# Linear-attention layers with centred weights, the residual on TensorE and f32r parts

## What is computed

```
q = phi(h @ wq + bq);  k = phi(h @ wk + bk);  v = h @ wv + bv
kv = sum over the sequence of k v;  z = 1 / (q . sum of k + 1e-6)
att = q kv z                                  (per head)
h = ln(h + att @ wo + bo, g1, be1)
y = gelu(h @ w1 + c1) @ w2 + c2
h = ln(h + y, g2, be2)
```

## Time and profile before

| | us |
|---|---|
| median of three runs | 2196.71 |
| lowest, highest | 2192.24, 2207.43 |
| profiled execution, its own time | 2191.62 |
| its span in the trace | 2189.9 |
| TensorE busy | 1866.5 |
| VectorE busy | 1437.3 |
| ScalarE busy | 1302.0 |
| GpSimd busy | 581.3 |

### The profile page before, as it was taken

The page is one execution under the profiler, slowest core; times in us unless marked ns, Lnnn a source line. Parts: engine busy times, 40 slices in busy tenths (PEclk is TensorE's granted clock), DMA queues, the critical chain, the costliest instruction groups (busy, mean ns, idle before and its releaser), DMA issues.

```text
span 2189.9 us, 23815 instructions
## 1 busy us (share of the span) xinstructions
PE 1866.5 (85%) x8305; PEld 1056.7 (48%) x8324; DVE 1437.3 (66%) x2318; ACT 1302.0 (59%) x2022; POOL 581.3 (27%) x685
## 2 busy tenths in 40 slices
PE   8999999999999989998677777997677677777998
PEld 6886444344434437885233334784122323332786
DVE  6886564456445647886755653886899755662787
ACT  6997555555555558997255556555644535556554
POOL 1443000000000002443522222222599612223221
PEclk9999999999999999999689998998799779999999
DMA  3221000000000002220000000200000000000110
GB/s 97 79 69 56 1 17 17 0 17 17 17 0 17 10 10 71 71 73 29 1 1 1 1 1 1 78 29 0 10 3 31 1 1 1 1 1 1 52 55 19
DMA packets 23746, 52.39 MB, mean 24 GB/s; under 512 B 2336, under 2 KB 6816, under 8 KB 23648
## 3 DMA queue, kind: packets, MB, share of 16 engines
q1 hardware_dynamic: 23648, 51.12, 7.3%
HBM read 49.47 MB, written 1.64 MB: 23 GB/s over the span
## 4 chain that ended last, share of the span: by engine, by line
PE 57%; DVE 21%; ACT 14%; issue 4%; POOL 2%; DMA 1%; ACTq 0%; POOLq 0%; DVEq 0%; SPq 0%
PE ps L440 9%; PE ps L442 9%; PE ps L441 9%; PE ps L708 5%; DVE arena L1463 5%; PE ps L225 4%; DVE arena L1208 4%; PE ps L701 4%; PE ps L928 3%; PE ps L898 3%; ACT rstd L242 2%; PE ps L887 2%; ACT arena L990 2%; ACT arena L1040 2%; ACT rstd L238 2%
## 5 line engine op out<-in xcount | busy, mean ns | idle before, releaser
L548 DVE TENSOR_TENSOR hid_lo<-arena,hid_hi 128x512 fp32r<-128x512 f32 x384 | 340.6, 900 | 67.1 <-ACT arena L498 64.7
L526 POOL TENSOR_TENSOR w_lo<-wslot,w_hi 128x512 fp32r<-128x512 f32 x56 | 77.5, 1389 | 759.4 <-DVE w_hi L543 759.4
L1208 DVE TENSOR_REDUCE arena<-ps 128x1 f32<-128x512 f32 (+3 forms) x352 | 213.2, 638 | 88.8 <-PE ps L902 85.7
L440 PE MATMUL ps<-x_hi,w_hi 128*128 128x512 f32 x512 | 208.1, 406 | 0.6 <-DVE arena L630 0.6
L441 PE MATMUL ps<-x_lo,w_hi 128*128 128x512 f32 x512 | 205.2, 401 | 0.0
L442 PE MATMUL ps<-x_hi,w_lo 128*128 128x512 f32 x512 | 205.0, 400 | 0.0
L495 ACT ACTIVATE hid_hi<-ps,wslot 128x512 fp32r<-128x512 f32 x256 | 177.1, 692 | 34.1 <-PE ps L442 6.3
L1040 ACT ACTIVATE arena<-ps 128x1024 f32<-128x1024 f32 (+3 forms) x256 | 166.5, 706 | 48.5 <-PE ps L918 47.9
L1126 POOL TENSOR_SCALAR_AFFINE_SELECT arena<-arena 128x256 f32<-128x256 f32 x256 | 102.2, 406 | 330.7 <-ACT arena L1040 328.2
L898 PE MATMUL ps<-arena 128*128 128x128 bf16 (+3 forms) x498 | 132.5, 332 | 65.3 <-DVE arena L1208 37.1
L498 ACT ACTIVATE arena<-ps,wslot 128x512 f32<-128x512 f32 x256 | 175.1, 684 | 0.0
(11 more groups left out here) (225 smaller groups left out, 3863.7 us busy)
## 6 DMA issues: line engine op xcount, KB each, us to landing
arena<-gates_dram SPq DMA_DIRECT2D x96, 256.0 KB, 3.5
wslot<-pack_a SPq DMA_DIRECT2D x16, 514.5 KB, 3.7
wslot<-pack_b SPq DMA_DIRECT2D x8, 901.5 KB, 4.6
wslot<-pack_c SPq DMA_DIRECT2D x8, 768.0 KB, 4.5
res<-x_in SPq DMA_DIRECT2D x4, 256.0 KB, 4.5
out_dram<-res SPq DMA_DIRECT2D x4, 256.0 KB, 2.9
bc_dram<-arena SPq DMA_DIRECT2D x1, 384.0 KB, 3.2
arena<-bc_dram SPq DMA_DIRECT2D x16, 24.0 KB
```

The lines of the kernel that those rows point to most:

```text
L440: pe.matmul(ps[:, bank, :], w1, hi, start=start, stop=False)
L548: dve.tensor_tensor(hid_lo[item % 2][:, k, :], hid32[:, k, :], hid_hi[item % 2][:, k, :].bitcast(F32), ALU.subtract).then_inc(S["hid_ok"], 1)
L1208: dve.tensor_reduce(neg_max[:, i, heads[0]:heads[-1] + 1:step], ps[:, bank, 0:len(heads) * keys].rearrange("p (m k) -> p m k", k=keys), AX ...
```

## The change

The layers are written out one after the other instead of looped, and the work of a layer is arranged anew.

- The residual goes through TensorE. The matrix `cent` (identity minus 1/128) is applied to the old state in two f32r parts (`centred`, two matmuls per sequence), and the product of the branch is added in PSUM. VectorE subtracts the row means from Wo and W2 once per layer (`weights`, steps 0 and 1), the biases bo and c2 are centred by one small matmul. What stands in PSUM is then already without its mean, and the norms have no mean matmul and no subtraction.
- Wo is folded into each sequence's key-value block: transpose (`kvt`), copy, a product of 128 columns with Wo (`g`), copy. The queries are multiplied by the spread reciprocals, and one matmul per sequence gives the branch. The denominators lie as 128 x 256, so that the reciprocal has 256 columns.
- The middle norm's variances of the four sequences stand in four strips of one bank; one Ln and one Exp serve all, and four matmuls with `pick` spread the root.
- Queries, up and down matmuls are three f32r matmuls each (`split3`). High parts of the state are written by ScalarE, low parts of the middle state by VectorE, low parts of the layer's output and of the weights by POOL (`pool_layers`, new). Gelu parts: for even pieces ScalarE writes gelu twice (f32r and f32), for odd pieces VectorE copies; VectorE subtracts.
- Order: keys and values of a sequence go ahead of its queries; up and down matmuls alternate piece by piece; the closing norm's variances stand between them, and that of the fourth sequence behind the next layer's first keys.
- SP's wait ahead of a layer's weights is now for the outputs of the layer that used the slot.

```diff
+            def split3(bank, w_at, s, hi, lo, lo_ready, stop, start=False):
+                w1, w2 = (t[s][:, w_at:w_at + P] for t in (wb_hi, w_lo))
+                pe.matmul(ps[:, bank, :], w1, hi, start=start, stop=False)
+                pe.matmul(ps[:, bank, :], w2, hi, start=False, stop=False)
+                lo_ready()
+                return pe.matmul(ps[:, bank, :], w1, lo, start=False, stop=stop)
...
+            def centred(bank, hi, lo, stop):
+                pe.matmul(ps[:, bank, :], cent_r[:, :], hi, start=True, stop=False)
+                return pe.matmul(ps[:, bank, :], cent_r[:, :], lo, start=False, stop=stop)
...
+                pe.wait_ge(S["w_parts"], c["parts"] + 2 * l + 2)
+                keys_values(0)
+                if l:
+                    last_var(l - 1)
+                queries(0)
+                queries(1)
+                keys_values(1)
+                queries(2)
+                keys_values(2)
+                queries(3)
+                keys_values(3)
+                for b in range(NB):
+                    pe.wait_ge(S["kf_ok"], m + b + 1)
...
+                for b in range(NB):
+                    pe.wait_ge(S["kvbd_ok"], m + b + 1)
+                    pe.transpose(ps[:, b, 256:256 + P], kv_bd[:, b, :], ident).then_inc(S["kvt_mm"], 1)
...
+                for b in range(NB):
+                    pe.wait_ge(S["kvt_ok"], m + b + 1)
+                    pe.matmul(ps[:, b, 384:384 + P], kv_t[:, b, :], w[:, B_WO:B_WO + P], start=True,
+                              stop=True).then_inc(S["g_mm"], 1)
...
+                def residual(b):
+                    pe.wait_ge(S["g_ok"], m + b + 1)
+                    centred(b, h_hi[:, b, :], h_lo[:, b, :], False)
...
+                pe.wait_ge(S["root_ok"], 2 * l + 2)
+                for b in range(NB):
+                    pe.matmul(ps[:, 4 + b, :], ccol("pick")[32 * b:32 * b + 32], root[32 * b:32 * b + 32, :],
+                              start=True, stop=True).then_inc(S["root_bc"], 1)
...
+                        pe.wait_ge(S["gelu_ok"], 16 * l + n - 2)
+                    split3(n % 3, B_W1 + k * P, s, mid_hi[:, b, :], mid_lo[:, b, :],
+                           lambda: pe.wait_ge(S["mid_lo_ok"], m + b + 1), True, True).then_inc(S["ff1_mm"], 1)
...
+                def ff2(b, k):
+                    if k == 0:
+                        centred(4 + b, mid_hi[:, b, :], mid_lo[:, b, :], False)
+                    pe.wait_ge(S["gelu_lo"], 16 * l + FC * b + k + 1)
+                    mm = split3(4 + b, B_W2 + k * P, s, hb_b[b % 2][:, k, :], lb_b[b % 2][:, k, :],
...
+                for item in range(NB + 1):
+                    for k in range(FC):
+                        if item < NB:
+                            ff1(item, k)
+                        if item:
+                            ff2(item - 1, k)
+                        if item == 2 and k == 1:
+                            pe.wait_ge(S["mid_xc"], m + 4)
+                            var(l, 0, LN2_BANK[0])
+                        if item == NB and k < 2:
+                            pe.wait_ge(S["gelu_ok"], 16 * l + 14 + k)
+                            var(l, 1 + k, LN2_BANK[1 + k])
...
+                mid_high(0)
+                mid_high(1)
+                gelu(0, 0)
+                mid_high(2)
+                mid_high(3)
+                gelu(0, 1)
+                gelu(0, 2)
+                gelu(0, 3)
+                for b in range(1, NB):
+                    for k in range(FC):
+                        gelu(b, k)
+                        if b >= 2 and k == 0:
+                            square(b - 2)
+                act.preload_act_table_set("natural_log_exp_and_others")
+                root_of(l, 0, LN2_BANK[0])
+                square(2)
+                root_of(l, 1, LN2_BANK[1])
+                out_high(l, 0, w)
+                root_of(l, 2, LN2_BANK[2])
+                out_high(l, 1, w)
+                square(3)
+                out_high(l, 2, w)
...
+            def weights(l, step):
+                s = l % 2
+                if step == 0:
+                    dve.wait_ge(S[f"w_in{s}"], w_count(c, l))
+                    square_w = wslot[:, s, B_WO:B_KVB].rearrange("p (a n) -> p a n", n=P)
...
+                    square_w = wslot[:, s, B_WO:B_KVB].rearrange("p (a n) -> p a n", n=P)
+                    dve.wait_ge(S["w_prep"], 2 * l + 1)
+                    dve.scalar_tensor_tensor(out=square_w, in0=w_sum[:, :].unsqueeze(2).to_broadcast([P, 1 + FC, P]),
+                                             scalar=-1.0 / P, in1=square_w, op0=ALU.mult,
...
+                    dve.wait_ge(S["w_prep"], 2 * l + 2)
+                    dve.tensor_copy(wb_hi[s][:, a:b], wslot[:, s, a:b]).then_inc(S["w_hi_ok"], 1)
+            def scaled(l, b, bank, bias):
+                dve.wait_ge(S["brs_ok"], 4 * l + b + 1)
+                dve.scalar_tensor_tensor(out=rstd[:, b, :], in0=ps[:, bank, :], scalar=bias, in1=rstd[:, b, :],
...
+                keys_values(0)
+                if l:
+                    scaled(l - 1, 3, 7, c_bias[:, LAYERS + l - 1:LAYERS + l])
+                    shifted(2 * m - 4, 3, ha, before[:, B_G2:B_G2 + 1], before[:, B_BE2:B_BE2 + 1], S["h_ok"])
+                queries(0)
+                queries(1)
+                keys(0)
+                keys_values(1)
+                queries(2)
+                keys_values(2)
+                keys(1)
+                queries(3)
+                keys_values(3)
+                keys(2)
+                keys(3)
...
+                if l + 1 < LAYERS:
+                    weights(l + 1, 0)
+                dve.wait_ge(S["den_ok"], l + 1)
+                dve.reciprocal(rz, rz).then_inc(S["rz_ok"], 1)
+                if l + 1 < LAYERS:
+                    weights(l + 1, 1)
...
+                    dve.wait_ge(S["gelu_ok"], n + 1)
+                    if b >= 2:
+                        dve.wait_ge(S["ff2_mm"], m + b - 1)
+                    if k % 2:
+                        dve.tensor_copy(hb_b[b % 2][:, k, :], hid_g[:, b % 2, k, :]).then_inc(S["gelu_hi"], 1)
+                        dve.wait_ge(S["gelu_hi"], 8 * l + 2 * b + k // 2 + 1)
+                    dve.tensor_tensor(lb_b[b % 2][:, k, :], hid_g[:, b % 2, k, :],
+                                      hb_b[b % 2][:, k, :].bitcast(F32), ALU.subtract).then_inc(S["gelu_lo"], 1)
...
+                for b in range(NB):
+                    for k in range(FC):
+                        gelu_low(b, k)
+                        if l + 1 < LAYERS and b == 1 and k % 2:
+                            weights(l + 1, 2 + k // 2)
+                c2 = c_bias[:, LAYERS + l:LAYERS + l + 1]
+                for b in range(NB - 1):
+                    scaled(l, b, 4 + b, c2)
+                    shifted(2 * m + 4, b, ha, w[:, B_G2:B_G2 + 1], w[:, B_BE2:B_BE2 + 1], S["h_ok"])
...
+            def weights(l, cut):
+                s, (a, b) = l % 2, CUTS[cut]
+                pool.wait_ge(S["w_hi_ok"], c["parts"] + 2 * l + cut + 1)
+                pool.tensor_tensor(w_lo[s][:, a:b], wslot[:, s, a:b], wb_hi[s][:, a:b].bitcast(F32),
+                                   ALU.subtract).then_inc(S["w_parts"], 1)
...
+                pool.tensor_tensor(h_lo[:, b, :], ha[:, b, :], h_hi[:, b, :].bitcast(F32),
+                                   ALU.subtract).then_inc(S["h_lo_ok"], 1)
...
+            for l in range(LAYERS):
+                for b in range(NB):
+                    low(l, b)
+                if l + 1 < LAYERS:
+                    weights(l + 1, 0)
+                    weights(l + 1, 1)
...
-            with sp.Fori(1, LAYERS // 2) as r:
-                l = 2 * r
-                for s in range(2):
-                    sp.wait_ge(S["ln_out"], 4 * (n0 + 2 * (l + s) - 4) + 8)
-                    sp.dma_start(wslot[:, s, 0:B_COLS], pairs[s, r]).then_inc(S[f"w_in{s}"], 16)
...
+            for l in range(LAYERS):
+                s = l % 2
+                if l < 2:
+                    slot_free(sp, s)
+                else:
+                    sp.wait_ge(S["h_hi_ok"], 4 * l)
+                    sp.wait_ge(S["h_ok"], 4 * l - 4)
+                sp.dma_start(wslot[:, s, 0:B_COLS], pack_b[l]).then_inc(S[f"w_in{s}"], 16)
```

480 lines of the change are left out of this document (303 added, 177 removed).

## The result

The changed kernel takes 2146.44 us (median of 4 runs, 2143.80 to 2149.48) against 2202.07 (4 runs of the kernel before, 2192.24 to 2208.88). The ratio is 0.975, with a 95% interval of 0.970 to 0.980. The forecast was 2132, its range 2110 to 2154. The profiled execution took 2143.8 (span 2142.1) against 2191.6.

The account below looks back on a forecast made before the run. TensorE was taken to bound stage B, the linear-attention layers, except at norms and a reciprocal. Start +9.4, cold clock +2, seven periods -68.0, tail -6.3 give -62.9: 2128.7 us, 2133.8 as median, taken as 2132 (2110 to 2154).

Parts of the forecast that it names:

- first period, with the cold clock: Stage's first layer: 61.3 us, with nothing left over from a layer before, plus 2 for a clock pause.
- tail: Stage's end, behind the seven periods: 81.7 us against 88.0, so -6.3.
- Keys, queries and their products: Head of each layer: 15.4 us of TensorE work plus 3.2 of waits, 18.6 against 17.6.
- Attention: Attention part of each layer: Wo folded in, reciprocal halved to about 1.7 us; 9.5 against 11.25.
- Middle norm: Norm ahead of the feed-forward: no mean or subtraction, one Ln and Exp for all sequences; 5.9 us against 7.59.
- Feed-forward: Feed-forward of each layer: split matmuls 22.2 us, residual 1.9, three variances 2.6, waits 2.5; 29.2 against 28.54.
- Closing norm: Layer's end: hidden behind the last feed-forward products and the next layer's first keys; 7.6 us of the gain.
- A: Rival: clock falls once per layer, in the middle norm; 14 us at most, 2146; chance 0.13 at its long end.
- B: Rival: the clock doesn't come back before the feed-forward ends; a layer takes 74.3 us, the kernel 2220; chance 0.04.
- C: Rival: POOL's six low parts all on the path, +8.1 us a layer, 2197, no change; chance 0.05.
- D: Rival: VectorE and ScalarE keep up better, the head's 3.2 us of waits go; 2106; chance 0.05.
- The prediction's own signs: In the layers: wrong if split matmuls stand further apart, clock is under 0.95, or POOL waits exceed 0.5 us a layer.

Follow-up runs that it names:

- e1_fill: The changed kernel with idle f32r products added where TensorE waits in the middle norm; 2144.71 us (2 runs).
- e7_border_fill: e3_norm_back with idle products added where TensorE waits at the layer's border and in the middle norm; 2167.4 us (2 runs).
- e3_norm_back: The changed kernel with the last sequence's variance, root and output put ahead of the next layer's first keys; 2183.61 us (10 runs), ratio to before 0.993.
- e4_f32_ff: The changed kernel with one f32 product in place of three f32r ones in the feed-forward, parts still made; 2185.01 us (7 runs), ratio to before 0.994.
- e6_pool_twice: The changed kernel with another, unread subtraction ahead of each of POOL's in the layers; six periods average 65.80 us against the changed kernel's 64.40.
- e5_before_again: The kernel before, unchanged, profiled once more; stage B 603.38 us from norm to norm, against 603.45 in its first profile.

## Why the prediction was right, and where it was off

The direction, the size and the mechanism held. From profiled execution to profiled execution 15.1 us are missing (2143.8 against 2128.7): 5.0 in stage B and 10.1 in the stages that the change doesn't touch. In the median 14 are missing (2146.4 against 2132).

| term | forecast | measured | from |
|---|---|---|---|
| first keys later | +9.4 | +8.8 | 17.57 (227.83 - 210.26) against 8.80 |
| first period, with the cold clock | 61.3 + 2 | 63.13 | its row |
| six periods | 63.2 each | 64.40 each | 386.43 / 6 |
| tail | 81.7 | 80.26 | 757.65 - 677.39 |
| stage B | -62.9 | -57.9 | 547.39 against 605.26 |
| all other stages | 0 | +10.1 | -47.8 of span |

1. *Keys, queries and their products:* 18.76 for 18.6, with the waits where they were put (1.02 ahead of the third product, 1.3 forecast). Right.
2. *Attention:* 9.12 for 9.5. The reciprocal's size was right; its wait is 0.37, not 0.7. The doubled reciprocal shows that its cover is used up.
3. *Middle norm:* 6.14 for 5.9, with one Ln and Exp. The mechanism is right; the terms that the prediction lists for it add up to 5.7, not to the 5.9 that it uses.
4. *Feed-forward:* this is the term that was mis-sized, 30.5 to the forecast's 29.2. In e1_fill, at full clock, the period is 64.0 and its feed-forward 29.9, so 0.7 is missing without any clock. The waits at its start were put at 2.5 and come to 2.1 (4.85 from the first to the fifth up product, less twelve products at 0.231). What was left out is the wait for the third sequence's square, 0.7 idle and 0.85 by the starts around it. The rest is the products' spacing, 0.234 (35 of them from 267.20 to 275.38) where 0.231 was laid out, a hundred times over. The clock adds 0.4 on average.
5. *Closing norm:* that it can be hidden is confirmed, what it is worth alone is not. The prediction put 7.6 of the 9.3 on this norm. The border, where the fourth sequence's part is hidden, is worth 3.6 a layer plus the clock (e7_border_fill, e3_norm_back), and the f32r products are worth 4.9 (e4_f32_ff). That second gain is in the prediction's own sum (32 products at 0.86 are 27.5, in place of them 22.2), but its marks hid it, since the residual and the three variances moved into the same 29 us. The two together are 8.5, a little more than the 8.2 that a layer gained. It isn't shown what the first three sequences' roots behind the feed-forward, the missing means and the single Ln and Exp are worth, nor what the added work costs; no run undoes one of these alone.

*First period and start:* the prediction let the first layer be 1.9 shorter than the rest, as nothing is left over from a layer before, and put 2 us of cold clock on top. The 63.13 measured is close to that 63.3, but the two terms can't be told apart. The cold clock is there: sequence 0's keys take 3.2 (227.83 to 231.05), those of sequence 1 take 1.5 (232.66 to 234.20). How much of these 1.7 the waits behind them take up, no run shows. The tail's 81.7 stands in the prediction without a working; 80.26 was measured.

*Rivals.* A happened, in seven layers of eight, with the mechanism named and both prices in or next to the ranges given (0.15 for 3.4 us, 0.5 to 0.8 for 6.8, and 0.1 more by e1_fill's own delay). That the kernel came out at A's 2146 is chance: A has 14 us of falls in the stage, and they cost some 2.3. B did not happen: the clock came back within 6.8 us each time. Its price was too high as well. It lets half clock cost half its length, so that 18 us a layer decide; in e3_norm_back 16 us cost 3.4 against e7_border_fill, a fifth of their length. C is excluded by e6_pool_twice, and no wait of TensorE for POOL stands in the changed kernel's six periods. D did not happen; the head's waits are all there.

*The prediction's own signs:* none of those that would have proved it wrong came. The clock over the six periods is 0.96; in the three with a long fall it is 0.947, just under the 0.95 that it names.

*Around the stage:* two things were outside the sum. The profiled execution of before was among its fastest (2191.6, against medians of 2198.1 to 2203.9 in all series, e5_before_again among them), so adding 5 for the median was about half of the 10.5 that were due. Put on the median of before, 2202.1, the forecast's 62.9 would have given 2139.2: 7 of the 14 us are the choice of the base. And the unchanged attention stages came out 8 longer in the profiled execution of after, at a lower clock. By the medians the kernel gained 55.6, a little less than the 57.9 that stage B lost between the two profiles.

## What to carry to other kernels

- Lay the new order out engine by engine against a layout that reproduces the old one; here every mark up to the feed-forward was met to 0.4 us. But price each part by undoing it, not by the marks between which it stands, and undo all of it (the border run undid one sequence of four): a gain and an addition in the same stretch hide each other.
- A layer norm hidden at a loop's border is worth its chain and the clock that its idle stretch would have cost; 17.6 us of e3_norm_back's layers were the clock's alone. Idle products in such a stretch show within one run how much of a loss is the clock's.
- When one stage is changed, compare it stage by stage: an unchanged stage here moved by 3 us between two profiles of the same kernel and by up to 9 over all kernels, more than some of the effects looked for.
